# Four sorted edge gathers: groups of six chunks laid per node tile, against 131 fixed groups whose shared ones stay in their slots

## The reference

```python
dst = minimum((3125 * uniform(key, (100000,)) ** 2.0).astype(int32), 49999); _o = argsort(dst); src, dst = src[_o], dst[_o]
# part 1: three relational convolutions, R = 5 edge types (256 -> 256 -> 128 -> 128)
def rgcn_conv(x, src, dst, etype, W, root, bias):
    agg = segment_sum(x[src], dst * R + etype, num_segments=n * R)          # summed by destination and type
    agg = where(cnt[:, None] > 0, agg / maximum(cnt, 1.0)[:, None], 0.0)    # mean
    return einsum('nrd,rdk->nk', agg.reshape(n, R, -1), W) + x @ root + bias
...
# part 2: attention: exp(-leaky_relu(s1[src] + s2[dst])) * h[dst] summed by src, layer norm, elu
# part 3: segment_sum(edge_weight[:, None] * x[row], col) @ W.T + b
# part 4: segment_sum(edge_attr, col) beside x, a dense layer, layer norm, prelu, a second dense layer
```

## Time and profile before

| what | value |
| --- | --- |
| median of 3 runs | 6623.57 us |
| profiled execution, from its first to its last instruction | 5873.0 us |
| median less that span: what lies around the instructions, and the difference of one execution from another | 750.6 us |
| pass 0, first to last gather start | 427.3 to 1653.6 us |
| pass 1 | 1669.1 to 2882.9 us |
| pass 2 | 2900.1 to 4117.1 us |
| pass 3 | 4527.0 to 5697.6 us |
| POOL busy | 3778.2 us, 64% |

### The profile page before, as it was taken

How to read it: one execution, slowest core, us unless ns; L and a number is a source line. 1 busy time by engine, 2 the same in 40 slices (tenths; PEclk the granted TensorE clock), 3 DMA queues, 4 the chain that set the end, 5 groups by cost and what they waited for, 6 DMA issues and landing times.

```text
span 5873.0 us, 106093 instructions
## 1 busy us (share of the span) xinstructions
PE 4465.0 (76%) x21917; PEld 3159.6 (54%) x21920; DVE 3165.9 (54%) x7327; ACT 1113.9 (19%) x4209; POOL 3778.2 (64%) x3598
## 2 busy tenths in 40 slices
PE   4777777777777787788777777777564988888873
PEld 1335556666654455555544444555463666666653
DVE  5323333333257777777777777777686333333335
ACT  0111111111111111111111111111473111111112
POOL 0007777777667777777677777777132777777760
PEclk8777777777789999999999999999696555555556
DMA  2113333333322222222212222222241333333330
GB/s 87 45 60 95 100 100 101 105 102 105 102 62 53 55 71 71 71 87 79 84 47 59 59 65 64 70 70 81 87 167 62 98 99 98 99 99 100 99 79 11
DMA packets 289401, 476.81 MB, mean 81 GB/s; under 512 B 77934, under 2 KB 197872, under 8 KB 285696
## 3 DMA queue, kind: packets, MB, share of 16 engines
q0 software_dynamic: 127008, 289.24, 18.7%
q1 hardware_dynamic: 162368, 187.29, 9.2%
HBM read 399.12 MB, written 77.10 MB: 81 GB/s over the span
## 4 chain that ended last, share of the span: by engine, by line
DMA 42%; PE 34%; issue 11%; DVE 7%; POOL 3%; DVEq 1%; POOLq 1%; ACT 1%; SPq 0%; ACTq 0%
DMA msg_r<-y_tab,idx_r 32%; PE psum L1116 9%; DMA msg_r<-z_tab,idx_r 9%; PE psum L1093 6%; PE psum L1219 5%; PE psum L1220 3%; POOL msg_r L384 2%; PE psum L998 2%; DVE h_t L877 2%; PE psum L1134 1%; PE psum L1151 1%; PE psum L1105 1%; PE psum L1176 1%; PE psum L1088 1%; DVE h_t L881 1%
## 5 line engine op out<-in xcount | busy, mean ns | idle before, releaser
L384 POOL DMA_INDIRECT msg_r<-y_tab,idx_r x2646 | 2775.6, 1049 | 1331.9 <-issue 905.7
L1116 PE MATMUL psum<-shot_r,hotb_r 128*128 128x400 bf16 x7056 | 1498.8, 335 | 503.8 <-DMA msg_r<-y_tab,idx_r 480.9
L1116 PEld LDWEIGHTS psum<-shot_r,hotb_r 128*128 128x128 bf16 x7056 | 574.7, 98 | 1031.7 <-DMA msg_r<-y_tab,idx_r 578.2
L384 POOL DMA_INDIRECT msg_r<-z_tab,idx_r x882 | 903.2, 1024 | 349.0 <-issue 211.9
L790 DVE TENSOR_SCALAR shot_r<-iota_h,edge_g 128x1600 bf16<-128x1600 f16 x1764 | 1103.6, 680 | 0.0
L451 ACT COPY idx_r<-row_i 128x1 int32 x2628 | 502.9, 191 | 3026.6 <-DMA msg_r<-y_tab,idx_r 2909.8
L1093 PE MATMUL psum<-hot_r,msg_r 128*128 128x128 f32 x3528 | 726.9, 363 | 254.9 <-DVE hot_r L768 134.9
L1093 PEld LDWEIGHTS psum<-hot_r,msg_r 128*128 128x128 f32 x3528 | 608.8, 255 | 403.2 <-DMA msg_r<-y_tab,idx_r 228.8
L1219 PE MATMUL psum<-msg_r,shot_r 128*128 128x128 f32 x1764 | 659.6, 476 | 143.2 <-DMA msg_r<-z_tab,idx_r 100.0
L1219 PEld LDWEIGHTS psum<-msg_r,shot_r 128*128 128x128 f32 x1764 | 430.2, 303 | 351.4 <-DMA msg_r<-z_tab,idx_r 300.2
L1220 PE MATMUL psum<-msg_r,hot_r 128*128 128x128 f32 x1764 | 539.7, 408 | 0.0
(11 more groups left out here) (209 smaller groups left out, 3344.9 us busy)
## 6 DMA issues: line engine op xcount, KB each, us to landing
msg_r<-in_attr SPq DMA_DIRECT2D x882, 64.0 KB
msg_r<-y_tab,idx_r POOLq DMA_INDIRECT x2646, 2.6
count_tab<-w_s SPq DMA_DIRECT2D x50, 800.0 KB, 3.7
h_t<-count_tab SPq DMA_DIRECT2D x25, 1600.0 KB, 6.7
y_tab<-y_s SPq DMA_DIRECT2D x25, 640.0 KB, 2.9
y_tab<-y_s SPq DMA_DIRECT2D x50, 320.0 KB, 2.3
msg_r<-z_tab,idx_r POOLq DMA_INDIRECT x882, 2.6
w_s<-inv_rows SPq DMA_DIRECT2D x450, 1.2 KB
```

The source lines that it names most:

```text
L384: pool.indirect_dma_start(out=msg_r[:, q, 0:width], out_offset=None, in_=table, in_offset=bass.IndirectOffsetOnAxis(ap=idx_r[:, q:q + 1], ...
L1116: ins = T.matmul(psum[:, 4 + b, 0:CB], hotb_r[:, q, :], shot_r[:, q, b * CB:(b + 1) * CB], start=first, stop=last)
```

## The change

Groups are now fixed: group g is the chunks 6g to 6g+5, 131 groups for all edges, and a tile is given the range of groups that touch it. With this seed the tiles have 27, 12, 9, 8, 8, 6, 6, 6, 6, 5, 5, 5, 5, 4, 5, then nine times 4 and once 3 groups, 156 in all. Of the 24 borders between tiles 23 have one group in common. For such a group the first tile's last visit and the next tile's first visit use the same gathered rows: it is gathered once, and PE and DVE visit it twice. The last border is different: the last tile takes three groups from 128 on, of which 128 and 129 were the tile before's, and they are gathered again. So 133 groups are gathered in each pass and 156 visited.

`p` still counts visits; the new `g` counts gathers, and `p = g + kept`, where KEPT is the number of groups kept so far. DVE goes on by `p`; POOL, SP and ACT go by `g`; PE by both. `groups` gets ten rows in place of four, which DVE works out at the start of the kernel.

```diff
-CPP = 7
-CROWS = -(-E // (P * CPP))
-CHUNKS = CROWS * CPP
 U = 6
-COLS = CHUNKS + U - 1
+GROUPS = -(-E // (P * U))
+GPP = 2
+GROWS = -(-GROUPS // GPP)
+COLS = GROUPS * U
 LEAST = 3
...
-        P0, P1, CHUNK, LAST = range(4)
+        P0, P1, CHUNK, KEPT, G_FIRST, G_NEW, G_LAST, G_END, G_CHUNK, G_HELD = range(10)
...
-                p0, p1, chunk = (tile_range(sp, n, D) for n in (P0, P1, CHUNK))
-                with sp.Fori(p0, p1) as p:
+                new, end, chunk, kept = (tile_range(sp, n, D) for n in (G_NEW, G_END, G_CHUNK, KEPT))
+                with sp.Fori(new, end) as g:
+                    freed = sp.snap((g + kept) * U)
                     for q in range(U):
-                        sp.wait_ge(s_free[3], p * U + (q + 1))
+                        sp.wait_ge(s_free[3], freed + (q + 1))
...
             def gather(k, table, width):
 
                 bound = pool.to_reg(table.shape[0] - 1)
-                end = tile_range(pool, P1, TILES - 1)
-                with pool.Fori(1, end) as p:
-                    freed = pool.snap(p * U)
-                    for q in range(U):
-                        pool.wait_ge(s_free[k], freed + (q + 1))
-                        pool.wait_ge(s_idx[k], freed + (q + 1))
-                        pool.sem_inc(s_go, 1)
-                        pool.indirect_dma_start(
...
+                with pool.Fori(0, TILES) as D:
+                    new, end, kept = (tile_range(pool, n, D) for n in (G_NEW, G_END, KEPT))
+                    with pool.Fori(new, end) as g:
+                        freed, loaded = pool.snap((g + kept) * U), pool.snap(g * U)
+                        for q in range(U):
+                            pool.wait_ge(s_free[k], freed + (q + 1))
+                            pool.wait_ge(s_idx[k], loaded + (q + 1))
+                            pool.sem_inc(s_go, 1)
+                            pool.indirect_dma_start(
...
-            def group_sums(k, p, slot, chunk_sums, first=False, last=False):
-                after, landed = pe.snap(p + 1), pe.snap(p * 16)
+            def group_sums(k, g, kept, slot, chunk_sums, first=False, last=False):
+                p = pe.snap(g + kept)
+                after, landed = pe.snap(p + 1), pe.snap(g * 16)
...
-                    first, last = pe.snap(tile_range(pe, P0, D)), pe.snap(tile_range(pe, LAST, D))
+                    first, last, kept = (pe.snap(tile_range(pe, n, D)) for n in (G_FIRST, G_LAST, KEPT))
                     start(D, slot)
-                    group_sums(k, first, slot, chunk_sums, first=True)
+                    group_sums(k, first, kept, slot, chunk_sums, first=True)
                     if table is not None and type(D) is not int:
                         table(D - 1)
-                    with pe.Fori(first + 1, last) as p:
-                        group_sums(k, p, slot, chunk_sums)
-                    group_sums(k, last, slot, chunk_sums, last=True)
+                    with pe.Fori(first + 1, last) as g:
+                        group_sums(k, g, kept, slot, chunk_sums)
+                    group_sums(k, last, kept, slot, chunk_sums, last=True)
                     stop(slot)
```

More of the change, by code:

```diff
@@ L678, in _ @@
-            then(V.tensor_tensor(out=groups[:, CHUNK, 0:TILES], in0=rng_row[:, 3, 0:TILES], in1=r_first, op=ALU.add))
+            r_p0, r_p1, r_last, r_kept = (rng_row[:, n, 0:TILES] for n in (3, 4, 5, 6))
+            V.tensor_scalar(out=r_p0, in0=r_before, scalar1=1.0, scalar2=None, op0=ALU.add)
+            V.tensor_tensor(out=r_last, in0=r_before, in1=r_n, op=ALU.add)
+            V.scalar_tensor_tensor(out=r_p1, in0=r_before, scalar=1.0, in1=r_n, op0=ALU.add, op1=ALU.add)
+            V.memset(rng_row[:, 8, :], 0.0)
@@ new lines, in _ @@
+            then(V.scalar_tensor_tensor(out=rng_row[:, 7, 0:TILES], in0=r_first, scalar=-1.0, in1=r_n, op0=ALU.add, op1=ALU.add))
+            V.tensor_tensor(out=rng_row[:, 11, 0:TILES], in0=r_first, in1=r_p0, op=ALU.subtract)
+            then(V.tensor_tensor(out=rng_row[:, 8, 1:TILES], in0=rng_row[:, 0, 1:TILES], in1=rng_row[:, 7, 0:TILES - 1], op=ALU.is_equal))
+            then(V.tensor_copy(rng_row[:, 9, 0:TILES], rng_row[:, 8, 0:TILES]))
+            at, step = 9, 1
+            while step < TILES:
+                to = 6 if 2 * step >= TILES else 19 - at
+                V.tensor_copy(rng_row[:, to, 0:step], rng_row[:, at, 0:step])
+                then(V.tensor_tensor(out=rng_row[:, to, step:TILES], in0=rng_row[:, at, step:TILES],
+                                     in1=rng_row[:, at, 0:TILES - step], op=ALU.add))
+                at, step = to, 2 * step
@@ new lines, in _ @@
+            V.tensor_copy(groups[:, P0, 0:TILES], r_p0)
+            V.tensor_copy(groups[:, P1, 0:TILES], r_p1)
+            V.tensor_copy(groups[:, KEPT, 0:TILES], r_kept)
+            V.tensor_scalar(out=groups[:, CHUNK, 0:TILES], in0=rng_row[:, 11, 0:TILES], scalar1=float(U), scalar2=None, op0=ALU.mult)
+            V.tensor_tensor(out=groups[:, G_LAST, 0:TILES], in0=r_last, in1=r_kept, op=ALU.subtract)
+            V.tensor_tensor(out=groups[:, G_END, 0:TILES], in0=r_p1, in1=r_kept, op=ALU.subtract)
@@ new lines, in _ @@
+            V.tensor_tensor(out=rng_row[:, 9, 0:TILES], in0=r_p0, in1=r_kept, op=ALU.subtract)
+            then(V.tensor_tensor(out=rng_row[:, 10, 0:TILES], in0=rng_row[:, 11, 0:TILES], in1=r_kept, op=ALU.add))
+            V.tensor_copy(groups[:, G_FIRST, 0:TILES], rng_row[:, 9, 0:TILES])
+            V.scalar_tensor_tensor(out=groups[:, G_HELD, 0:TILES], in0=rng_row[:, 9, 0:TILES], scalar=-1.0, in1=rng_row[:, 8, 0:TILES],
+                                   op0=ALU.add, op1=ALU.add)
+            V.tensor_tensor(out=groups[:, G_NEW, 0:TILES], in0=rng_row[:, 9, 0:TILES], in1=rng_row[:, 8, 0:TILES], op=ALU.add)
@@ L679, in _ @@
+            then(V.tensor_scalar(out=groups[:, G_CHUNK, 0:TILES], in0=rng_row[:, 10, 0:TILES], scalar1=float(U), scalar2=None, op0=ALU.mult))
             dve.sem_inc(s_groups, 1)
```

86 lines of the change are left out of this document (41 added, 45 removed).

## The result

The changed kernel takes **6759.1 us** (median of 4 runs, 6756.7 to 6768.7), the kernel before on the same chip 6620.5 (4 runs, 6617.0 to 6639.0): a ratio of 1.0205, 95% interval 1.0185 to 1.0224, so 139 us slower. The forecast was +198 us, 6822 with a range from 6735 to 6925.

A forecast was written before the change was run, and what follows sets the result against it. The four passes were taken to go at POOL's gather pace. Gathers saved (−453) and stalls (+635) gave +182 us; counting +12, starts +3 and search +1 made +198: 6822 us, range 6735 to 6925.

The forecast's parts named there:

- kept-group interval: From a kept group's first gather to the next group's: 18.9, 14.5, 14.5, 14.85 us, against 7.8 to 8.3 ordinarily.
- counting stage and search: Nine more group visits in the counting stage, +12 us, and the search at the kernel's start, +1 us.
- Fewer gathers, −453, against stalls, +635: 84 gathers less per pass save 453 us; POOL waiting at kept groups for their slots costs 635 us.
- The length from the rows of before: Kept interval read off the old trace's border: 13.07 us in pass 1, plus 0.86 for POOL's answer and 0.6 for registers.
- The term for registers: Extra register load and operations on the path between tiles: 0.6 us a kept group, bounds 0 and 1.0.
- the paces of the rows would leave the sum as it is: Second visits' one-hots fall where POOL stands, possibly saving 21 us in passes 1 and 2; not taken into the sum.
- The landing: Gather's issue to landing at a kept border: trace's 2.79 us used; the skill's fit would take 46 us off the sum.
- The rival that the second visit hides: POOL keeps its pace over borders while the second visit runs, so −453 stays: 6187 us; chance of faster 7%.
- POOL's new loop: Register loads per tile or the operation ahead of each gather not hidden: 1.5 us a border, +138, 6960 us; 12%.
- The clock: PE's clock falls in passes 1 and 2, +92: 6915 us, 6%; or is better in pass 0: 6730 us, 5%.
- the median is 750.6 above it, and I take that part as unchanged: Time beyond the profiled span of 5873.0 us taken as unchanged, so span 6071 and time 6822 us.
- Three of the signs: Named signs: 798 gathers per pass, border idle about 6.5 us (11 in pass 0), none elsewhere, unchanged tile pace, pass 0 longer.

The follow-up runs named there:

- e6: The changed kernel with group ranges held as unsigned 16-bit numbers, no assertions on loads, on a chip without stops: 6059.5 us, 1.0311 to the kernel before.
- e5: The kernel before with group ranges held as unsigned 16-bit numbers, no assertions on loads, on a chip without stops: 5874.2 us, 0.9993 to the kernel before.
- e10: The kernel of e6 run again on a third chip, without stops: 6054.7 us, 1.0305 to the kernel before.
- e9: The kernel of e5 run again on a third chip, without stops: 5870.6 us, 0.9989 to the kernel before.
- e4: e2 with two copies of the gathered rows in pass 2 alone, POOL's loop there written out: 6106.3 us, 131 below e2.
- e8: e6 with two copies of the gathered rows in all four passes, gather loops written out with constants: 5483.0 us, 0.9326 to the kernel before.
- e2: The changed kernel with bounds assertions on its register loads, but for those of chunk numbers: 6237.4 us, 1.061 to the kernel before.
- e12: e5 plus a SyncE loop raising an unawaited semaphore 320 times per tile in pass 1, chip with stops: 6866.5 us, kernel before 6538.0.
- run 14: Not a run label: in the result's run of the changed kernel (6759.1 us), 14 of pass 1's 23 kept borders have 14.4 to 14.8 us.
- e11: e8 with no group kept, all 156 visits gathered anew: 6064.9 us, 1.0323 to the kernel before.
- e1: The kernel before with bounds assertions on its register loads of group numbers: 5896.3 us, 1.003 to the kernel before.

## Why the prediction was right, and where not

The range, the sign and the mechanism held. On two chips without stops each step of the sum can be read, e6 against e5 (first gather and pass lengths from the rows above; e5 has passes of 1220.1, 1211.4, 1212.9 and 1178.8 us, and its first gather at 423.8):

| step | forecast | e6 − e5 | e10 − e9 |
| --- | --- | --- | --- |
| kept-group interval, passes 0 to 3 | 18.9, 14.5, 14.5, 14.85 | 18.07, 14.54, 14.60, 14.90 | 18.29, 14.54, 14.60, 14.92 |
| pass 0 | +83 | +84 | +75 |
| pass 1 | +27 | +21 | +17 |
| pass 2 | +26 | +18 | +21 |
| pass 3 | +46 | +44 | +44 |
| counting stage and search | +13 | +9 | +10 |
| starts of passes 1 to 3, attention included | +3 | +7 | +5 |
| span of the profiled execution | +198 | +183 | +172 |
| median of the runs | +198 | +185 | +184 |

The steps add up to the spans; a profiled execution lies up to 15 us off the median of its runs (e6's 6044.2 and 6059.5).

- *Fewer gathers, −453, against stalls, +635.* Right. e4 and e8 took the single copy away and most of the stall went with it. In pass 0 two errors cancel, which is luck. The 18.3 us put all that was left of the pass on the borders; in the trace of before a border's two groups take 17.90 us in the mean (7.82 and 10.08), and the others, the start left out, 7.93 where the sum has 7.82. So the stall is 0.6 to 0.8 us shorter than forecast and the group behind it 0.5 to 0.6 longer (8.42 and 8.33 us), and the pass comes out at 1303.7 and 1307.2 us for 1309.3.
- *The length from the rows of before.* Its parts add up in pass 1: 13.07 + 0.86 + 0.6 is 14.53, and 14.54 was measured. The term for registers (0.6 us, bounds 0 and 1.0) can be read from the same place of both traces, PE's first root matmul of the new tile, before and in e6:

```profile
2061.11 0.48 PE L1127 MATMUL psum<-ones,b_s 1*128 1x128 f32 x2 [0.36 <-issue]
...
2077.99 0.48 PE L1157 MATMUL psum<-ones,b_s 1*128 1x128 f32 x2 [0.84 <-issue]
```

  PE stands 0.48 us longer before it. In the mean of pass 1 from the close to the end of slot 0 are 2.61 us before and 3.09 in e6. So the term is some 0.5 us, and the loads lie on the path; e2's assertions behind them add another 1.4 us a border.
- *Passes 1 and 2 were forecast 6 and 8 us too long.* The step is "the paces of the rows would leave the sum as it is". The group behind a kept one takes 7.99 and 8.04 us, where the group in the same place, the new tile's second, takes 8.34 and 8.45 in e5: 23 × 0.35 and 23 × 0.41 are 8 and 9 us. The Trainium skill, "SBUF — State Buffer" (Who interferes with whom), lets an instruction of VectorE in some modes lock POOL out of a shared port; by it the one-hots that fall where POOL stands free its gathers, and the prediction worked out 21 us for that. The trace bears out the sign and some 17 of the 21, though not which port it was. In e5's pass 1, 273 of 882 gathers take over 1.10 us, and DVE's comparison that writes 16-bit masks (L793) runs during each of them, as it does during 331 of the shorter ones; in e6 212 of 798 are so long.
- *The landing.* The measured 14.54 us goes with the 2.79 of the earlier trace rows; in e6 the median from issue to landing is 2.8 us in pass 0 and 2.6 in pass 1. The fit of the Trainium skill, "DMA: Bandwidth & Descriptors" (Anatomy of one DMA), gives a gather of pass 1 (64 KB) 2.0 us and 0.15 for the bytes, by which the interval would be an estimated 13.9; the prediction's 0.3 is that of pass 0's 128 KB. That page's advice (Rules for kernel authors), to issue early and wait late, is what e8 does, and the 577 us agree with it.
- *The rival that the second visit hides* is refuted for one copy: POOL stood 6.5 us at the borders. With two copies it comes true but for 2 to 3.4 us at small tiles. *POOL's new loop* is refuted: the kept interval of pass 1 is 14.54 us and not 1.5 more, and inside tiles a group takes 8.23 us in e6 against 8.30 in e5. *The clock*: the granted clock is 1.00 of 2.4 GHz in pass 1 and 0.58 in pass 3 of e6 (0.99 and 0.54 before), so it didn't fall, and it is 0.75 in pass 0 of both, so it didn't rise there either.

```profile
1754.30:2986.60 1232.30, 1006.30 (x5856) 663.88 (x5857) 968.25 (x1882) 194.17 (x888) 845.63 (x797) 1.00 0.22 64
4644.50:5866.90 1222.40, 1036.76 (x3897) 813.86 (x3898) 418.94 (x928) 161.92 (x840) 822.76 (x798) 0.58 0.31 85
```

(These are e6's stretches of passes 1 and 3, with the columns of the earlier trace rows.)

**The step that failed** is the one that made a time of the sum: "the median is 750.6 above it, and I take that part as unchanged". The 750 us lie in the gather passes, as stops: e12 shows them there for the kernel before, though beside times of 6538 us; where it takes 6620, no profile of it was made. They did not stay unchanged: the result's run of the changed kernel has 6759.1 − 6059.5 = 700 us of them, where the kernel before has 6620.5 − 5874.2 = 746, so the change costs 139 there and 185 elsewhere. Two things can have taken those 46 us. The stops go with the gathers (90, 81 and 76 in passes 0, 2 and 3 of e12, without the 20 of pass 0's borders, and 86, 67 and 68 in the changed kernel), and 9.5% fewer gathers would make 746 into 675. And a stop that falls into a stall costs nothing: of pass 1's 23 kept borders in the result's run 14 have 14.4 to 14.8 us, as undisturbed ones have, the others 15.5 to 18.7. The runs don't tell the two apart. That 6759 still lies in the range is partly luck: its bounds came from registers, landing and clock, and none of these made the 46 us. Three of the signs that the prediction named (idle above 4 us, pass 0 longer, 798 gathers) came out as written. The others, the pass lengths, no such idle time elsewhere and the pace inside a tile, hold in e6 (1304, 1232, 1231 and 1222 us) and not in the result's run, because of the stops and not of the change.

## What to carry to other kernels

Leaving out a transfer gains only if the engine that issues them can run on. Here the group that was kept blocked its own six slots for two visits, and the length of that stall could be read to 0.1 us from the border that was already there; with a second copy of the slots the same change turned from +185 to −391 us against the same control, of which the second copy and the written-out loops give some 138 without it (e11). And compare the span of a profile with its own time before calling the difference an overhead: 750 us that seem to lie outside may be those of a slower chip.

## What the runs showed of the hardware

- The kernel before takes 5879, 5879 and 5875 us on three chips, 6538 and 6620 us elsewhere. In the profiles from there (e12, and the result's run of the changed kernel) POOL stands for about 2 us at about one of nine to twelve gathers, and DVE and ACT have idle times near it, though not in the same instant; stages without gathers (attention 408 to 411 us, tail 175 to 176) are as long as elsewhere.
- In the result's run the recorded instructions and semaphore events come to 22.9, 23.6, 22.9 and 23.1 per us in the four passes, though their work differs; in executions without stops they come to 32 to 48. What is missing is semaphore events (36,552 of e6's 85,117), not instructions. It suggests that the recording of the execution has to do with the stops. That is argued from the counts alone; e12, which was to test it, made SyncE late, and reached 27 to 31 per us where SyncE added records, so a fixed total of 23 is not the limit.
- An assertion behind a register load costs 0.9 to 2.3 us at each border where three such loads lie on the path of a stall. In the kernel before all of them cost 17 us: e1's profile has 23 more than e5's ahead of the first gather and 30 in pass 0, and 10 and 13 less in passes 1 and 2, where fewer gathers are over 1.10 us long (239 for 273 in pass 1). The two profiles differ by 31 us, more than the medians.
